# Graph layer sums on one core: 128-node windows summed as two column tiles of 64 nodes instead of four of 32

## Reference

```python
norm = -dinv[src] * dinv[dst]                      # dinv = 1/sqrt(out-degree)
def prop(h):
    return segment_sum(h[src] * norm[:, None], dst, num_segments=6250)
def cheb_conv(h, W0, W1, b):
    return h @ W0 + prop(h) @ W1 + b
h = relu(layernorm(x))
h = cheb_conv(h, W1_0, W1_1, b1)
h = layer_norm(h, gamma, beta)
h = where(h >= 0, h, 0.01 * h)
out = x + cheb_conv(h, W2_0, W2_1, b2)
```

## Time and profile before

| | us |
|---|---|
| median of 3 runs | 2083.98 (2083.77 to 2084.26) |
| the profiled execution | 2083.35 |
| its span, first to last instruction | 2081.5 |
| PE busy | 1742.9 (84%) |
| POOL busy | 1506.8 (72%) |
| DVE busy | 774.1 (37%) |
| ACT busy | 316.4 (15%) |
| mean granted clock of TensorE | 0.986 |

### The profile page before, as it was taken

The page is one execution under the profiler, slowest core; times in us unless marked ns, Lnnn a source line. Parts: engine busy times, 40 slices in busy tenths (PEclk is TensorE's granted clock), DMA queues, the critical chain, the costliest instruction groups (busy, mean ns, idle before and its releaser), DMA issues.

```text
span 2081.5 us, 25826 instructions
## 1 busy us (share of the span) xinstructions
PE 1742.9 (84%) x8692; PEld 669.5 (32%) x8692; DVE 774.1 (37%) x2405; ACT 316.4 (15%) x647; POOL 1506.8 (72%) x1596
## 2 busy tenths in 40 slices
PE   3559888888888888888888888888988888988888
PEld 3433333333223333323333333332332333333333
DVE  9844444444444444444442222221222222222211
ACT  7801111111111111111111011100111000110000
POOL 2277777777777777777777777777777777777774
PEclk9999999999999999999999999999999999999999
DMA  9898888888888888888878888888888888888885
GB/s 252 275 324 257 243 241 242 242 241 242 236 237 242 241 242 242 237 236 241 242 227 260 249 253 256 255 251 252 252 254 255 251 256 253 249 257 254 252 249 157
DMA packets 188683, 514.94 MB, mean 247 GB/s; under 512 B 45240, under 2 KB 46927, under 8 KB 187308
## 3 DMA queue, kind: packets, MB, share of 16 engines
q0 software_dynamic: 128576, 422.78, 69.2%
q1 hardware_dynamic: 56374, 90.16, 12.5%
q10 hardware_dynamic: 3608, 0.42, 0.3%
HBM read 472.40 MB, written 40.84 MB: 247 GB/s over the span
## 4 chain that ended last, share of the span: by engine, by line
POOL 61%; issue 21%; PE 10%; DVE 5%; DMA 1%; ACT 0%; SPq 0%; DVEq 0%; ACTq 0%
POOL arena L557 61%; PE ps L1222 4%; PE ps L1346 2%; DVE w_all L834 2%; PE ps L1385 1%; DVE work L834 1%; PE ps L1214 1%; DMA scal<-node_scales 1%; DMA arena<-table,idx_all 0%; DVE ps L1091 0%; ACT arena L684 0%; DVE stats L1094 0%; PE ps L1372 0%; DVE ps L1101 0%; PE ps L1261 0%
## 5 line engine op out<-in xcount | busy, mean ns | idle before, releaser
L557 POOL DMA_INDIRECT arena<-table,idx_all x1536 | 1453.7, 946 | 472.5 <-issue 468.0
L1346 PE MATMUL ps<-arena,hots 128*32 128x512 f32 x4940 | 707.4, 610 | 148.9 <-DVE hots L1013 79.2
L1346 PEld LDWEIGHTS ps<-arena,hots 128*32 128x32 f32 x4940 | 179.5, 110 | 651.1 <-issue 457.6
L1013 DVE TENSOR_SCALAR hots<-iota_f,loc_all,arena 128x64 f32<-128x64 f32 (+2 forms) x768 | 232.9, 331 | 346.2 <-DMA arena<-table,idx_all 344.6
L1222 PE MATMUL ps<-arena 128*128 128x512 f32 (+1 forms) x432 | 196.5, 597 | 35.8 <-ACT arena L684 35.8
L1222 PE MATMUL ps<-w_all,arena 128*128 128x512 f32 (+1 forms) x432 | 196.1, 597 | 35.8 <-ACT arena L684 35.8
L674 ACT ACTIVATE arena<-ps,scal 128x512 f32<-128x512 f32 x106 | 72.9, 688 | 929.3 <-PE ps L1372 888.3
L1222 PE MATMUL ps<-arena,work 128*128 128x512 f32 (+1 forms) x432 | 195.6, 595 | 0.0
L1222 PE MATMUL ps<-w_all,work 128*128 128x512 f32 (+1 forms) x432 | 192.2, 588 | 0.0
L1130 DVE SCALAR_TENSOR_TENSOR ps<-ps,scal,arena 128x512 f32<-128x512 f32 x52 | 39.5, 759 | 346.3 <-PE ps L1222 346.3
L1022 DVE TENSOR_SCALAR hots_next<-iota_f,loc_next 128x32 f32<-128x32 f32 x51 | 13.6, 267 | 395.7 <-PE ps L1372 395.7
(11 more groups left out here) (159 smaller groups left out, 766.2 us busy)
## 6 DMA issues: line engine op xcount, KB each, us to landing
arena<-table SPq DMA_DIRECT2D x106, 256.0 KB, 4.0
arena<-table,idx_all POOLq DMA_INDIRECT x1550, 3.9
table<-arena SPq DMA_DIRECT2D x53, 256.0 KB, 4.1
arena<-in_x_dram SPq DMA_DIRECT2D x53, 256.0 KB, 4.9
out_dram<-arena SPq DMA_DIRECT2D x53, 256.0 KB
table<-arena SPq DMA_DIRECT2D x10, 1124.4 KB
arena<-in_x_dram POOLq DMA_DIRECT2D x9, 1120.0 KB, 35.3
w_all<-in_L_gnn_W_dram SPq DMA_DIRECT2D x2, 1024.0 KB, 12.0
```

What stands on the lines that cost most here:

```text
L557: nc.gpsimd.indirect_dma_start(out=rows_of(n, c)[0:rn, 0:RW if L == 0 else D], out_offset=None, in_=table[L][0:NEAR if near else N, :], in ...
L1013: hot = nc.vector.tensor_scalar(hot_of(n, c)[:, cols], iota_f[:, cols], loc, factor_of(i, c), ALU.is_equal, ALU.mult)
L1346: return nc.tensor.matmul(tx_ps[n % 2][strip, :], hot_of(n, c)[:, strip], rows_of(n, c)[:, 0:D], start=start, stop=stop)
```

## The change

`Q` becomes 64: two strips of 64 nodes, the first over slots 0 to 9, the second over 7 to 14 (and the next chunk's first slot). The rounds go from 7 to 10, with the second strip two rounds behind. The one-hots get 64 columns, or 128 for the slots 7 to 9, which belong to both strips; those of the last chunk have 128 columns as before. Of the six slot edge tests two are left. They are those of before at node 64 (slots 7 and 10), so a list that held the plan of before holds this one.

```diff
-    Q = 32
-    STRIPS = ((0, 5), (3, 10), (7, 14), (10, SLOTS))
-    BOUNDS = ((3, False, 1), (5, True, 1), (7, False, 2), (10, True, 2), (10, False, 3), (14, True, 3))
-    ROUNDS = 7
+    Q = 64
+    STRIPS = ((0, 10), (7, SLOTS))
+    BOUNDS = ((7, False, 1), (10, True, 1))
+    ROUNDS = 10
...
-                strips = strips_of(c) if i < NC - 1 else [0, 3]
+                strips = strips_of(c) if i < NC - 1 else [0, 1]
...
-                    for t in range(4):
+                    for t in range(2):
                         c0, c1 = STRIPS[t]
                         c1 = min(c1, slots_of(i))
-                        c = c0 + r - (t == 3)
+                        c = c0 + r - 2 * t
...
-                            last = strip_sum(L, i, t, c, c == c0, c == c1 - 1 and not (t == 3 and follows))
+                            last = strip_sum(L, i, t, c, c == c0, c == c1 - 1 and not (t == 1 and follows))
```

## The result

| | before | after |
|---|---|---|
| median, measured together (20 runs each) | 2082.72 us | 2085.29 us |
| ratio | | 1.0013, 95% [1.0007, 1.0019] |
| profiled execution, its span | 2083.35, 2081.5 us | 2084.68, 2082.5 us |

The change costs 0.13% (2.57 us). That is clear of the scatter of these runs, but inside the 0.2% that the prediction had set as no difference. The forecast was 2084.2 us. Part of its closeness is luck: it was counted from a median before of 2083.98, so it was a change of +0.2 us, and the kernel before took 1.3 us less when both were measured together.

A forecast was written before the change was run, and what follows sets the result against it. POOL's gather issues (18.44 us a chunk) were taken to bound the kernel, hiding PE's 17.58. 2083.35 + 0.36 - 0.85 + 0.7 = 2083.6 us, or 2084.2 for the median, no difference; the case's range 2082 to 2088, overall 2081.5 to 2092.

The forecast's parts named there:

- POOL sets the pace, 1.250 us a gather, PE's longer sums are hidden: Both layers: POOL needs 18.44 us for a mean chunk, 0.86 us more than PE's new cycle of 17.58.
- the threshold: PE's cycle in layer 0: above 17.86 us PE isn't in step at the layer's end; every tenth costs 5 us.
- Sums 8.74 us, cycle 17.58 in both layers, in step from chunk 35, 8 chunks into layer 1: PE's sums and whole cycle per chunk, and when PE makes up its late start of 29.1 us in layer 0, 7 in layer 1.
- The upper half starts within 0.1 us of the lower: PE's sums: the upper half's first matmul, behind three others, starts early, so its 18 records fit beside the lower half's 20.
- Late landings +0.7 us: Both layer ends: less slack per chunk may leave PE late there; +0.7 us taken from between 0 and +4.
- Wider one-hots: 0 us: DVE's one-hots: none grows by over 0.053 us, 0.8 us a chunk at most, covered by waits for landings; 0 taken.
- The flag, taken as 0: POOL's idle before 119.17 us: at most 0.7 us could go with an earlier flag; 0 taken.
- Layer 0's end +0.36: Layer 0, chunk 51: PE's 8.38 us become 8.74 and POOL's restart at 1101.25 follows, +0.36 us.
- The end of layer 1, clock -0.85: PE behind layer 1's last gather: 2.4 GHz instead of 1.2 saves up to 1.7 us; half, -0.85, taken.

The follow-up runs named there:

- e9: The changed kernel with every strip matmul of 64 x 512 issued as two of 64 x 256; 2107.33 us, ratio 1.0130 to the kernel before.
- e4: The changed kernel with the upper half over slots 6 to 14 instead of 7 to 14; 2484.57 us against 2631.17 before on a slow chip, ratio 0.9459.
- the control: The kernel before, unchanged, measured as if it were a change; 2081.48 us against 2083.25, ratio 0.9997.
- e6: The changed kernel with all ten lower-half matmuls ahead of the upper half (layer 1's first chunk excepted); 2704.97 us against 2631.17 before on a slow chip, ratio 1.0276.
- e5: The changed kernel with all six slot edge tests of before; 2470.39 us against 2631.17 for the kernel before on a slow chip, ratio 0.9394.

## Why the prediction was right, point by point

- **POOL sets the pace, 1.250 us a gather, PE's longer sums are hidden**: right. No wait of POOL for PE; e9 shows what is past the threshold.
- **Sums 8.74 us, cycle 17.58 in both layers, in step from chunk 35, 8 chunks into layer 1**: right; 8.79, 17.6, chunk 35, chunk 7.
- **The upper half starts within 0.1 us of the lower**: wrong, 0.92 us. I read "may start early" from a strip that stood behind six matmuls, without seeing that these were two for each strip. The result stood because 18 records need 0.86 us less than 20, and the delay costs no more than 0.05 us of sums. One slot more in the upper half (e4) would have made it cost 0.86 us.
- **Late landings +0.7 us**: not seen. The wait at the boundary grew by 0.2 us. Behind the last gather five executions on fast chips took 18.1 to 20.6 us, the narrow ones 20.56 and 18.81 and the changed one 19.33, so no row shows such a term there, and times that scatter like this can't rule out 0.7 us.
- **Wider one-hots: 0 us, "on an engine that waits for landings"**: this is the step that missed the 2.6 us. I asked only what they cost DVE (0.05 us each, covered), and took POOL's 1.250 us as given. POOL's issues beside one-hots take 1.1 to 1.3 us more in each layer, in layer 1 beside those of 128 columns, in layer 0 beside those of 64 as well. The rest of the +1.7 and +1.6 us is two collisions with two-input DVE instructions, 0.3 to 0.5 us each, and the 0.2 us of the boundary. That the width causes the first part is argued, as said above.
- **The flag, taken as 0**: before, the first L557 issue waited, 1.03 us of idle, and the control waits 1.05 us; now 0.30. From the first gather of all to 118.03 us POOL takes 18.42 us in place of 19.08: -0.7 us, the bound that I had named. In both traces of the kernel before this issue starts 2.16 us behind DVE's writing of the flag (the end of L825), and in the changed kernel 3.20 us behind it and with no wait: the flag no longer holds it up.
- **Layer 0's end +0.36**: POOL's wait at the boundary is 4.39 us against 4.16 and 4.12 (control): +0.2, and it stands inside the 1.7 us.
- **The end of layer 1, clock -0.85**: no row bears it as a gain. The changed kernel's last dense product runs at the upper level, 3.72 us in place of 4.62, and from its last gather to the end it takes 19.33 us against 20.56. But the control, with tiles of 32, runs at the upper level there as well (PEclk 1.00 from 2047.2 to 2050.5 us) and takes 18.8 us. The half-clock stretch of the earlier trace rows stood in one of two executions of the same kernel, and I had built a term on it.

Added up over whole executions, the changed kernel's span is 1.0 us over the first of the kernel before: -0.5 us ahead of the first gather, -0.7 to L557, +1.7, +1.6, and -1.2 behind the last gather. Over the control's it is 3.0 us longer: -0.6, -0.7, +2.1, +1.7, +0.5. The two lie on both sides of the 2.57 us between the medians; single executions don't settle it closer. The forecast had +0.2 from terms that were mostly others. That the total came so near is in part luck; that it is no difference is not, since every term was small against a bound that was read rightly.

## What to carry to other kernels

When one engine issues every gather and sets the pace, ask of each edit what it does to the length of that engine's instruction, even an edit on an engine that is idle two thirds of the time: 2 ns in the mean of 1536 issues made the 3 us. And look for single instructions of DVE with both inputs in SBUF: a gather issue that starts behind one waits for nearly all of it. Lay out column tiles so that no tile's next matmul stands behind more than two of another tile, and count in matmuls, not in columns. And run a control, the kernel before as if it were a change: it took away a term that had been built on a clock reading of a single execution.

## What the runs showed of the hardware that I had not expected

- **TensorE looks two matmuls ahead in a tile.** Another tile's first matmul starts 0.9 us behind three matmuls of 128 x 512 (e4 and after), 6.92 us behind ten (e6), 1.79 us behind six half-width ones (e9). The Trainium skill, TensorE: Matmul & The Clock Gate, section on the mechanism of packing, has matmuls as a strict FIFO, monotone in start; these runs show starts out of the written order, within a short reach.
- **A DVE instruction with both inputs in SBUF holds up a gather issue on GpSimd that starts behind it**, by what is left of it less 0.12 to 0.13 us (33 of 34 issues); an issue that starts ahead of it isn't held up (54 of 54 within 0.01 us).
- **A DVE one-hot can lengthen a gather issue as well, by less.** To over 0.99 us it does so in 22 of 75 cases beside one of 128 columns in layer 1 of the changed kernel (by 0.14 us at most). Beside one of 64 columns it does in 4 of 108 cases in layer 1 of the kernel before, in none of 70 there after, and in 11 of 321 in layer 0 after.
- **Chips of one kind differ by 25% on the same program** (2593 and 2631 us against 2082 and 2083). On two of them PE stands still in gaps of 0.8 or 1.5 us that no wait explains. The same tiles, with the six slot edge tests kept (e5), take 6% off there, and the change costs 0.13% on the others, so a verdict on a kernel with many small PE instructions holds for the chip on which it was measured.
